# Edge slots in a graph network's sort: VectorE adds a unit's two masked halves, TensorE sums one of them

## What is computed

```python
edge_index = jnp.stack([src, dst])
x = x + gnn0(_layernorm(x), W, bias, src, dst, edge_weight)      # h = x @ W; segment_sum(h[dst] * weight, src)
x = x + moe0(_layernorm(x))                                      # 8 experts, top 2
x = x + gnn1(_layernorm(x), edge_index, edge_weight, ...)        # 3 layers with batch norm
x = x + moe1(_layernorm(x))                                      # shared expert and 8 experts, top 2
```

## Time and profile before

| | us |
|---|---|
| median of 3 runs (2925.08 to 2926.45) | 2925.66 |
| the profiled execution | 2918.11 |
| its span | 2916.3 |
| PE busy in the span | 2338.1 |
| DVE busy in the span | 1261.8 |
| POOL busy in the span | 1412.0 |

### The profile page before, as it was taken

How to read it: one execution, slowest core, us unless ns; L and a number is a source line. 1 busy time by engine, 2 the same in 40 slices (tenths; PEclk the granted TensorE clock), 3 DMA queues, 4 the chain that set the end, 5 groups by cost and what they waited for, 6 DMA issues and landing times. The chain is left out here.

```text
span 2916.3 us, 52084 instructions
## 1 busy us (share of the span) xinstructions
PE 2338.1 (80%) x13974; PEld 2094.8 (72%) x13974; DVE 1261.8 (43%) x3577; ACT 932.4 (32%) x2684; POOL 1412.0 (48%) x1484
## 2 busy tenths in 40 slices
PE   6999689888869667776567775667765899999999
PEld 5899678887768446676366765467664799999988
DVE  6499866664443434343434443434433532111121
ACT  3688678784112240000210000300002423333322
POOL 2777677773024527777247776077773011111041
PEclk8999889999769888987788897888986699999999
DMA  2100133332349623333133333133332359999922
GB/s 75 48 3 4 33 94 104 104 104 47 79 141 342 187 91 105 105 105 104 36 104 104 104 105 95 44 105 105 105 105 49 89 199 327 325 328 326 310 80 61
DMA packets 245494, 363.30 MB, mean 125 GB/s; under 512 B 59545, under 2 KB 190594, under 8 KB 244994
## 3 DMA queue, kind: packets, MB, share of 16 engines
q1 hardware_dynamic: 175376, 194.92, 20.6%
q0 software_dynamic: 66752, 163.74, 20.2%
q10 hardware_dynamic: 3250, 3.20, 0.4%
HBM read 322.49 MB, written 38.72 MB: 124 GB/s over the span
## 5 line engine op out<-in xcount | busy, mean ns | idle before, releaser
L827 POOL DMA_INDIRECT z_or_messages<-h_rows,agg_idx x768 | 729.3, 950 | 345.2 <-issue 224.9
L858 PE MATMUL ps<-z_or_messages 128*128 128x125 f32 x3072 | 482.4, 321 | 279.0 <-DMA z_or_messages<-h_rows,agg_idx 237.9
L858 PEld LDWEIGHTS ps<-z_or_messages 128*128 128x128 f32 x3072 | 448.5, 231 | 318.0 <-issue 253.2
L800 ACT CAST agg_idx<-slots 128x4 int32 x264 | 51.7, 196 | 1033.9 <-PE ps L858 573.9
L885 DVE TENSOR_TENSOR h_features<-h_features,ps 128x250 f32 x384 | 159.2, 415 | 508.7 <-PE ps L858 461.5
L1460 POOL DMA_INDIRECT moe_room<-h_rows,moe_inverse x112 | 105.8, 945 | 555.7 <-PE ps L1550 391.9
L827 POOL DMA_INDIRECT agg_room<-h_rows,agg_idx x256 | 248.7, 972 | 96.1 <-issue 67.5
L1719 ACT ACTIVATE moe_room<-ps,moe_b 128x128 f32<-128x128 f32 x560 | 162.7, 367 | 364.9 <-PE ps L1562 364.9
L1562 PE MATMUL ps<-moe_room 128*128 128x128 f32 x2240 | 273.0, 277 | 6.7 <-DVE moe_room L1771 4.0
L1562 PEld LDWEIGHTS ps<-moe_room 128*128 128x128 f32 x2240 | 260.5, 193 | 13.4 <-issue 5.8
L608 POOL DMA_INDIRECT payloads<-pay_st,idx_st x208 | 208.5, 1002 | 117.6 <-DMA idx_st<-slot_i 61.2
(11 more groups left out here) (296 smaller groups left out, 3266.0 us busy)
## 6 DMA issues: line engine op xcount, KB each, us to landing
moe_room<-in_L_ffn_W1p_dram SPq DMA_DIRECT2D x56, 1024.0 KB, 6.9
moe_room<-in_L_ffn_W2p_dram SPq DMA_DIRECT2D x56, 1024.0 KB, 7.3
moe_room<-in_L_ffn_w_dram SPq DMA_DIRECT2D x112, 256.0 KB, 4.9
expert_out<-moe_room SPq DMA_DIRECT2D x112, 128.0 KB, 5.7
z_or_messages<-h_rows,agg_idx POOLq DMA_INDIRECT x768, 2.8
h_rows<-moe_xn SPq DMA_DIRECT2D x10, 625.0 KB
h_rows<-layer_rows SPq DMA_DIRECT2D x48, 128.0 KB, 1.7
agg_room<-h_rows,agg_idx POOLq DMA_INDIRECT x256
```

Of the source, the lines that this page charges most:

```text
L827: self.pg.nc.gpsimd.indirect_dma_start(self.G[:, k, :], None, self.pg.H, bass.IndirectOffsetOnAxis(ap=self.idx[:, k:k + 1], axis=0)).then_ ...
L858: last = nc.tensor.matmul(out[:, c, :], self.G[:, k, c * 128:(c + 1) * 128], self.S[:, k, :], start=(u == 0), stop=(u == PAIR - 1))
```

## The change

The masked halves are no longer both sent to PE. DVE adds them (`add(n)`, one fp32 add of 208 or 192 columns into a new ring `both`, 4 buffers), and `summed(n)` is one fp32 matmul. The add of unit n-1 is issued behind the multiply of unit n; the last unit of each q has its add right behind its multiply. A new semaphore `s_mask` counts multiplies and releases `rank`; `s_part` now counts adds, releases `summed`, and frees the ring of masked halves; `s_red` frees the ring of sums.

```diff
+        both = sb("pair_slots", [P, PARTS, widest])
+        s_mask = sem("masked")
...
+        def both_of(n):
+            return both[:, n % PARTS, 0:SORTED[n // UNITS][1] - SORTED[n // UNITS][0]]
...
+                def add(n):
+                    dve.wait_ge(s_mask, n + 1)
+                    if n >= PARTS:
+                        dve.wait_ge(s_red, n - PARTS + 1)
+                    v.tensor_tensor(both_of(n), part_of(n)[:, 0, :], part_of(n)[:, 1, :], ALU.add).then_inc(s_part, 1)
...
                         dve.wait_ge(s_pre, n + 1)
                         if n >= PARTS:
-                            dve.wait_ge(s_red, n - PARTS + 1)
-                        v.tensor_tensor(part_of(n), prefix(n), onehots(n), ALU.mult).then_inc(s_part, 1)
+                            dve.wait_ge(s_part, n - PARTS + 1)
+                        v.tensor_tensor(part_of(n), prefix(n), onehots(n), ALU.mult).then_inc(s_mask, 1)
+                        if n > q * UNITS:
+                            add(n - 1)
+                    add((q + 1) * UNITS - 1)
                     dve.wait_ge(s_red, (q + 1) * UNITS)
...
                 def rank(n):
                     first, end = SORTED[n // UNITS]
                     if n >= 2:
-                        pe.wait_ge(s_part, n - 1)
+                        pe.wait_ge(s_mask, n - 1)
...
                 def summed(n):
                     pe.wait_ge(s_part, n + 1)
-                    for u in range(2):
-                        last = nc.tensor.matmul(reduced(n // UNITS), pg.ident[0:P, 0:P], part_of(n)[:, u, :],
-                                                start=(n % UNITS == 0 and u == 0),
-                                                stop=(n % UNITS == UNITS - 1 and u == 1))
-                    last.then_inc(s_red, 1)
+                    nc.tensor.matmul(reduced(n // UNITS), pg.ident[0:P, 0:P], both_of(n), start=(n % UNITS == 0),
+                                     stop=(n % UNITS == UNITS - 1)).then_inc(s_red, 1)
```

## The result

| | before | with the change |
|---|---|---|
| median, us | 2924.31 (20 runs, 2920.14 to 2932.72) | 2918.98 (20 runs, 2914.81 to 2926.39) |
| ratio | | 0.9984, 95% interval 0.9977 to 0.9991 |
| the profiled execution, its span | 2918.11, 2916.3 | 2924.35, 2922.5 |

The kernel is faster by 0.16%, 5.3 us between the medians; 4.0 us was forecast. Two more sets of runs of the same kernel gave 0.9996 and 0.9988, so the gain is nearer 3.5 us (0.12%, the three ratios weighted by their runs) than 5. The interval of the second set (0.9987 to 1.0005) does not exclude that nothing was gained, so the time alone is weak evidence and the stage has to carry the argument. Note that the profiled execution after is 6.2 us *longer* than the one before. Single executions of one kernel differ by 12 us here, so spans can't be compared; the stage has to be read by itself, from its first `rank`.

A forecast was written before the change was run, and what follows sets the result against it. The scatter leg, which waits for q = 0, was taken to bound the sorting stage. Head 0.93, steady part 2.5 and end 0.6 sum to 4.0 us: 2925.66 - 4.0 = 2921.7 us, range 2917 to 2926.5.

The forecast's parts named there:

- What bounds the stage: End of the sorting stage: the scatter leg sets the merge's start, by 1.06 us; q = 1 is not on it.
- The add: DVE, each unit of q = 0: one new add of 208 columns, taken as 0.374 us from another instruction's row.
- The chain: Loop through DVE and PE in q = 0, add(n) to add(n+2): 1.895 us for two units, setting the pace.
- `summed` to `rank`: PE step of the loop in q = 0: 0.41 us, being 0.36 plus 0.05 because PE comes out of idleness.
- The sum for q = 0: All of q = 0: 0.93 + 2.5 + 0.6, a gain of 4.0 us.
- head: First units of q = 0, PE at the lower clock, which rises at the same time as before: gain 0.93 us.
- steady part: q = 0 from rank(5) to rank(24): 19 units at 0.95 instead of 1.08 us, a gain of 2.5 us.
- end: q = 0 from rank(24) to DVE's read of the sums: 2.80 instead of 3.40 us, a gain of 0.6 us.
- q = 1: Second sorting part: 21 norm units lose 0.33 us each, to 1.76 us; all becomes DVE idle before the merge, some 9 us.
- The scatters: POOL's indirect DMAs keep number and gaps; slowing by the adds under q = 1 taken as 0, 1.2 us kept for the range.
- lose its clock: Rival: PE's gaps of 0.24 us in q = 0 drop its clock to the lower level; about 2932 us, chance 5%.
- The looser chain: Rival: some step overlaps, only DVE's own bound rules q = 0, pace 0.785 us, gain 7.1 us, 2918.6 us; chance 10%.

The follow-up runs named there:

- q0_only: The change with the DVE add only in q = 0, q = 1 summing both halves on PE as before; ratio to the kernel before 0.9988.
- q1_only: The change with the DVE add only in q = 1, q = 0 as in the kernel before; ratio to the kernel before 0.9997.
- late_again: Second set of the same kernel as `late_sum`; ratio to the kernel before 0.9974.
- late_sum: The changed kernel with PE summing one unit later, unit n-1 after rank(n+2); ratio to the kernel before 0.9981.
- again: The changed kernel run once more, unaltered; ratio to the kernel before 0.9996.
- again_2: The changed kernel run a third time, unaltered; ratio to the kernel before 0.9988.
- own_add: The changed kernel with each unit's add right behind its own multiply, not behind the next one; ratio to the kernel before 0.9987.

## Why the prediction was right

**What bounds the stage.** Right, and shown by the pair `q0_only` and `q1_only`: only q = 0 is on the way to the merge.

**The add.** 0.374 us was taken from a row of another instruction; the 25 adds of 208 columns took 0.366 us each:

```profile
L680 DVE TENSOR_TENSOR part_slots<-ps,onehots 125x416 f32<-125x416 f32 x25 | 14.7, 589 | 4.6 <-PE ps L742 4.4
...
L668 DVE TENSOR_TENSOR pair_slots<-part_slots 125x208 f32<-125x208 f32 x25 | 9.1, 366 | 0.0
```

**The chain.** 1.895 us for two units was forecast, 1.94 us measured. The steps, forecast and measured: add to `summed` 0.425 and 0.42; `summed` to `rank` 0.41 and 0.45; `rank` to multiply 0.56 and 0.56; multiply to add 0.50 and 0.51. The second was mis-sized by 0.04 us, and its reason was too narrow. `summed` to `rank` takes 0.45 us behind PE's wait, but also 0.43 us at 47.95, where no wait stands ahead, against 0.36 us for two of these instructions before. In both the weight load (PEld) starts only 0.01 to 0.03 us ahead of its matmul; before, and in `late_again`, it starts 0.09 us ahead, and there the step is 0.36 and 0.37 us. That fits a load that has to wait for the add; no run separates it. That DVE starts an instruction before the last has ended (0.50 us, then 0.28 us) holds; by the whole durations DVE alone would need 0.589 + 0.366 = 0.955 us a unit, and `late_sum` runs at 0.785. So the Trainium skill's sentence about the pipe that must be empty (VectorE: DVE Perf Modes, The DRAIN you can't avoid) does not describe these instructions. The same section excepts a next instruction that is not held, without a number; here it starts 0.08 to 0.09 us before the end of the one ahead.

**The sum for q = 0.** 4.0 us forecast, 4.24 us in this profile: head 1.40 (0.93 forecast), steady part 20.52 - 18.23 = 2.29 (2.5), end 3.40 - 2.85 = 0.55 (0.6). The sum comes so close because a head that was too small and a steady part that was too large offset each other. The head is the term that moves. In the other two profiles of the change the read came 1.1 us later, at 27.6 us, a gain of 3.2 us, and there the clock rises later. A window of the change's profile:

```profile
38.00:39.00 1.00, 1.00 (x9) 0.82 (x7) 0.55 (x2) 1.00 (x5) 0.00 (x0) 1.00 0.00 0
```

and the same one of `again`:

```profile
38.00:39.00 1.00, 1.00 (x5) 0.94 (x4) 0.41 (x1) 1.00 (x5) 0.00 (x0) 0.50 0.00 0
```

The granted clock was at its lower level until about 37.9 us in the first, 38.6 us in the kernel before, and 41.0 us in `again` and `again_2`, 3.6, 5.6 and 6.8 us after the first `rank`. I had let it rise at the same time as before; that it rose earlier in this profile is chance, since the same kernel did the opposite twice. `late_sum` and `late_again` differ in the same way (3.3 and 6.6 us), and `q1_only`, whose q = 0 is that of the kernel before, rose at 6.5 us and has its read 0.45 us later.

**q = 1.** 21 units at 1.76 us were forecast: at 75.66 and 77.42 us stand two `rank`s with a norm step between them.

```profile
75.66 0.33 PE L739 MATMUL ps<-onehots,tri 125*125 125x384 f16 x1
...
77.42 0.33 PE L739 MATMUL ps<-onehots,tri 125*125 125x384 f16 x1
```

The idle time ahead of the merge is 9.45 us (some 9 forecast).

**The scatters.** From the first scatter to the last start it is 270.59 us before (308.18 - 37.59) and 270.69 us after (304.04 - 33.35). The 25 adds of q = 1 slow them by no more than 0.1 us together.

**The rivals.** PE did not lose its clock: 1.00 in the steady part of q = 0. But the case was milder than the rival supposed: it had gaps of 0.24 us in every 0.95, and PE waited 0.18 us once in 1.94 us and shows 4.46 us of 5 as busy. (The share that I gave for the norm steps, 1.09 us of 1.46, is not the busy share that the profile shows there either: the earlier trace rows has 7.86 us of 9.) The Trainium skill tells of a clock that swings with PE's short idle gaps (TensorE: Matmul & The Clock Gate, A second HAM failure mode: psum-queue depth-cycling); these gaps did not bring that about, and longer ones were not tried. The looser chain at 0.785 us did not occur in the change, but it is what `late_sum` makes of it. That the time moves by 0.14%, within what the measurement can tell, was right in size (0.16%, 0.04% and 0.12%). The median of the 20 runs lies 2.7 us under the forecast of 2921.7: 1.35 us of it is that the kernel before measured 2924.31 and not 2925.66, the rest that the medians lie 5.3 us apart and not 4.0, more than the stage gained (3.9 us) and more than in the two later sets.

## What to carry to other kernels

When work moves from the bounding engine to one with time to spare, add up the chain of waits that goes round both engines, not only each engine's load: here PE saved 0.36 us a unit and the pace gained 0.11, and moving one in-order instruction back by one place freed another 0.19. Look at which leg the work is on before counting its gain: half of this change was on a leg with slack, and once four columns were moved into the slack, the merge came 2.7 to 5.2 us earlier still, about as much as the change itself had brought. Where single executions differ by more than the effect, count from a landmark in the stage and compare there.

## What the runs showed of the hardware

The clock's rise moves the head of a stage by more than I had thought, and the window's granted clock does not show it at the start of a program. In 18 to 20 us PE works on the same 50 counting matmuls in both kernels; windows of that line alone, before:

```profile
18.00:20.00 2.00, 2.00 (x14) 1.49 (x13) 1.00 0.98 167
```

and with the change:

```profile
18.00:20.00 2.00, 2.00 (x8) 1.30 (x7) 1.00 1.13 196
```

Fourteen matmuls against eight in 2 us, and a clock of 1.00 printed for both (in 16 to 18 us it is eight in both kernels, again with 1.00); the first `rank` then starts at 33.02 us or at 34.38 us. This part of the code is the same in both kernels, and `own_add`, with the same code there too, had its first `rank` at 32.98 us. So 1.4 us of a profile's span is decided before the changed lines are reached, by when the faster matmul spacing sets in.
